# A Perceiver layer on one core: scores by pairs of heads, a fused decay and maximum, quantization shared with GpSimd, and the tail's weights loaded early

## The reference

```python
x = x + cross_attention(layernorm(x), ctx)        # 16 heads of 64, 4096 keys, biases, @ Wo + bo
x = x + self_attention(layernorm(x))              # 16 heads of 16, 256 keys
x = x + ffn(layernorm(x))                         # 256 -> 704 -> 256, silu(gate) * up
# self_attention
latent = (x @ W_k + x @ W_v) @ W_down_kv          # 64 wide
k, v   = latent @ W_up_k, latent @ W_up_v
scores = (q @ k.T) / sqrt(256) * exp(-0.01 * |i - j|)
out    = softmax(scores) @ v, all heads, @ W_o
# ffn: every product has both operands quantized to FP4 and back, in blocks of 16 along the last dim:
scale = max(|block|) / 6;  q = nearest of {0, .5, 1, 1.5, 2, 3, 4, 6} to |x / scale|, with sign, * scale
```

## Time and profile before

| | |
|---|---|
| runs | 1412.96, 1418.12, 1417.87 us, median 1417.87 |
| profiled execution | 1414.05 us, its span 1412.1 us |
| TensorE busy | 1315.2 us, 93% of the span |
| VectorE, ScalarE, GpSimd busy | 1006.2, 870.5, 657.0 us |
| TensorE's mean granted clock | 0.973 |
| read from HBM | 20.85 MB |

### The profile page before, as it was taken

One profiled execution on the slowest core, in us unless ns is written; L12 is line 12 of the kernel. 1 busy time (PEld: TensorE's weight loads), 2 busy tenths in 40 slices (PEclk: granted clock), 3 DMA queues, 4 the chain that ended last, 5 costly groups with the idle time before them and its releaser, 6 DMA issues. The chain is left out here.

```text
span 1412.1 us, 24618 instructions
## 1 busy us (share of the span) xinstructions
PE 1315.2 (93%) x9284; PEld 1121.4 (79%) x9284; DVE 1006.2 (71%) x1375; ACT 870.5 (62%) x1700; POOL 657.0 (47%) x797
## 2 busy tenths in 40 slices
PE   5899999999999999999999999999999996589857
PEld 5788888888888888888888888888888885267734
DVE  3666678667866777678767876787678767299666
ACT  3667666676667666676667666766676663256511
POOL 5655755475547553565457545754574440000000
PEclk9999999999999999999999999999999999699879
DMA  4010000000000000110000000000000000300000
GB/s 127 16 45 2 16 1 9 8 16 1 9 9 31 16 24 31 38 31 9 2 23 1 8 2 23 1 9 1 9 1 1 1 9 1 101 0 1 1 0 15
DMA packets 24901, 22.95 MB, mean 16 GB/s; under 512 B 4432, under 2 KB 24528, under 8 KB 24784
## 3 DMA queue, kind: packets, MB, share of 16 engines
q1 hardware_dynamic: 24784, 21.38, 5.0%
HBM read 20.85 MB, written 0.52 MB: 15 GB/s over the span
## 5 line engine op out<-in xcount | busy, mean ns | idle before, releaser
L548 ACT ACTIVATE pT_hi<-psT 128x512 fp32r<-128x512 f32 x512 | 292.4, 601 | 237.6 <-PE psT L320 222.5
L623 DVE TENSOR_TENSOR pT_lo<-psT,pT_hi 128x512 fp32r<-128x512 f32 x512 | 330.3, 684 | 105.4 <-ACT pT_hi L548 104.9
L617 DVE TENSOR_REDUCE negm<-psS 128x1 f32<-128x1024 f32 x256 | 311.7, 1218 | 51.2 <-PE psS L310 51.2
L267 POOL TENSOR_TENSOR kT<-kraw,khi 64x512 fp32r<-64x512 f32 x252 | 324.9, 1289 | 0.0
L513 ACT ACTIVATE prob<-psS,negm 128x1024 f32<-128x1024 f32 x256 | 285.7, 1116 | 1.0 <-DVE negm L617 1.0
L320 PE MATMUL psT<-ident,prob 128*128 128x128 f32 x2048 | 268.5, 274 | 3.9 <-DVE pT_lo L623 3.9
L261 POOL CAST khi<-kraw 128x512 fp32r<-128x512 f32 x126 | 76.9, 610 | 418.0 <-ACT kraw L523 416.6
L336 PE MATMUL psO<-pT_hi,v 128*128 128x256 f32 x1024 | 268.5, 294 | 1.2 <-DVE pT_lo L623 0.4
L320 PEld LDWEIGHTS psT<-ident,prob 128*128 128x128 f32 x2048 | 233.1, 140 | 38.8 <-issue 11.1
L337 PE MATMUL psO<-pT_lo,v 128*128 128x256 f32 x1024 | 256.7, 283 | 0.0
L336 PEld LDWEIGHTS psO<-pT_hi,v 128*128 128x128 f32 x1024 | 196.2, 192 | 2.7 <-DVE pT_lo L623 2.6
(11 more groups left out here) (215 smaller groups left out, 1563.9 us busy)
## 6 DMA issues: line engine op xcount, KB each, us to landing
cst<-in_ctx_dram SPq DMA_DIRECT2D x12, 512.0 KB, 3.8
oT<-in_ctx_dram SPq DMA_DIRECT2D x4, 512.0 KB, 5.3
wraw<-in_L_xattn_Wk_dram SPq DMA_DIRECT2D x8, 256.0 KB, 2.7
wraw<-in_L_xattn_Wv_dram SPq DMA_DIRECT2D x8, 256.0 KB, 2.7
wraw<-in_L_xattn_Wq_dram SPq DMA_DIRECT2D x8, 256.0 KB, 2.7
wo<-in_L_xattn_Wo_dram SPq DMA_DIRECT2D x8, 256.0 KB, 2.8
ff_wdn<-in_L_ffn_w_down_dram SPq DMA_DIRECT2D x1, 704.0 KB, 8.2
ff_win<-in_L_ffn_w_gate_dram SPq DMA_DIRECT2D x1, 640.0 KB, 5.3
```

The lines of the kernel that those rows point to most:

```text
L267: pool.tensor_tensor(kT[half, m // 2 % KRING, h, 1, :], raw[own, :], khi[own, :].bitcast(F32), ALU.subtract).then_inc(k_split, 1)
L548: act.activation(pT_hi[:, i % PRING, :], psT[:, t % 2, :], ACT.Copy).then_inc(ph_ok, 1)
L617: dve.tensor_reduce(negm[:, g % 2, h, qt, c:c + 1], psS[:, qt, :], AX.X, ALU.max, negate=True)\
L623: dve.tensor_tensor(pT_lo[:, i % PRING, :], psT[:, t % 2, :], pT_hi[:, i % PRING, :].bitcast(F32), ALU.subtract).then_inc(pl_ok, 1)
```

## The change

**Loads.** A class `Tail` holds the second part's weights in the memory that the transposed context takes in the first part; SyncE loads them once the last key and value projections are done (`k_ps`, `v_ps` at N), and no longer at the start of the second part. GpSimd makes masks and distances there, ScalarE the decay in steps 125 and 126. The output bias is loaded in the first group, and GpSimd adds it to y in step 12.
**Merged weights.** GpSimd adds W_k and W_v, TensorE turns the sum and multiplies it by W_down_kv after the loop; the latent is then one product of x (`wc`), and `kvT` is gone.
**Last group.** Its quarters 0 to 5 are merged within steps 125 to 127, one head a step, with the weights for a head made by itself (`head_max`, `head_end`); the sums of these six are three additions on GpSimd. Quarters 6 and 7 stay behind the loop, on VectorE.
**Scores.** q is masked by parity only; a head is a product over 32 rows, and the pair of heads of `scores(p)` has different rows. There are four PSUM banks, two for a pair. Weight turning takes PSUM space of `saO` that is free at the time, with one buffer instead of two.
**VectorE.** Decay and maximum are one `tensor_tensor_reduce` for each half of the queries, and the negation is an operation of its own. **Quantization.** Operations 0, 1, 2, 3, 5 and 6 of a chunk stay on VectorE at fixed heads, 4, 7, 8 and 9 go to GpSimd, with two buffers. The first batch is normalized in iteration 19, the second at the end.

```diff
+    # first part, GpSimd
+    if n == FIRST + KT * FIRST:
+        pool.tensor_tensor(y[:, :, :], y[:, :, :], cst[:, 0, :]...to_broadcast([P, B * QT, D]), ALU.add)
+    def add_out(g, k):
+        pool.tensor_tensor(oweighed[:, 0:2, :], oweighed[:, 0:2, :], oweighed[:, 2:4, :], ALU.add)
+        pool.tensor_tensor(oweighed[:, 0, :], oweighed[:, 0, :], oweighed[:, 1, :], ALU.add)
+        pool.tensor_tensor(on[:, qt, h * HD:(h + 1) * HD], oweighed[:, 0, 0:HD], oweighed[:, 0, HD:2 * HD], ALU.add)
+    # first part, TensorE: steps of the last group, then behind the loop
+    elif k >= 13 and g + 1 == GP:
+        wait(pe, comb, 16 * g + 2 * (2 * (k - 13) - 1) + 1 if k > 13 else 0)
+        post(g, 2 * (k - 13), psW[:, :])
...
+    if g == GP - 1 and k >= 13:
+        wait(pe, comb, 16 * g + 2 * 2 * (k - 13) + 1)
+        post(g, 2 * (k - 13) + 1, psW[:, :])
...
-    for k in range(8):
-        post(GP - 1, k, dst)
+    post(GP - 1, 6, psW[:, :])
+    post(GP - 1, 7, bank_S[0])
+    for half in range(KT):
+        for kt in range(KT):
+            last = pe.transpose(bank_T[0][...], tail.w[:, 0, kt, half * P:(half + 1) * P], ident[:, :])
+    for kt in range(KT):
+        for half in range(KT):
+            last = mm(bank_T[1][...], tail.wkvT[:, half, kt * P:(kt + 1) * P], tail.wd[:, half, :], ...)
+    # first part, VectorE, steps 13 to 15 of the last group
+    weigh_out(g, 2 * (k - 13), psW[:, :])       # before p_low(n, 0)
+    weigh_out(g, 2 * (k - 13) + 1, psW[:, :])   # before p_low(n, 2)
+    head_end(k - 12)                            # at the end of steps 12 to 15
+    head_max(k - 11)                            # at the end of steps 11 to 14
     # second part, TensorE
-    for d in range(KT):
-        step(("kv", d), product([(w[:, i, kt, cols(d)], xnT[:, kt, :]) for i in range(2) for kt in range(KT)]))
+    step(("lat", 0), product([(wc[:, kt, :], xnT[:, kt, :]) for kt in range(KT)]))
...
+    HEADS = (0, 2, 1, 3, 4, 6, 5, 7, 8, 10, 9, 11, 12, 14, 13, 15)
+    def scores(p):
+        if p >= 2:
+            pe.wait_ge(top_ok, 4 * p - 4)
+        for qt in range(QT):
+            for u in (2 * p, 2 * p + 1):
+                b, h = u // H, HEADS[u % H]
+                at = h % HPT // 2 * 2 * HD
+                rows = slice(at, at + 2 * HD)
+                last = mm(banks[u % 4][:, qt, :], qm[rows, h % 2, h // HPT, r * P:(r + 1) * P],
+                          kT[rows, h // HPT, b * S:(b + 1) * S], start=True, stop=True)
+        last.then_inc(s_ok, 1)
     for i in range(U + 3):
-        if i < U:
-            scores(i)
+        if i % 2 == 0 and i < U:
+            scores(i // 2)
     # second part, VectorE
+    CHUNK_AT = (0, 4, 9, 13, 18, 22)
     for u in range(U):
-        for i in range(WPU * u, min(WPU * u + WPU, CHUNKS * OPS)):
-            weight_op(i)
-        dve.tensor_tensor(sd_[:, u % 2, :, :], psS[:, u % 2, :, :], decay[:, :, :], ALU.mult)
-        dve.tensor_reduce(negm[:, u, :], sd_[:, u % 2, :, :], AX.X, ALU.max, negate=True)
+        for c in range(CHUNKS):                 # ops 0 | 1, 2, 3 | 5, 6 at CHUNK_AT[c] + 0 | 1 | 3
+            ...                                 # op 5 waits for GpSimd's op 4
+        if u == H + 3:
+            normalized(0)
+        for qt in range(QT):
+            dve.tensor_tensor_reduce(sd_[:, u % 2, qt, :], banks[u % 4][:, qt, :], decay[:, qt, :], 1.0,
+                                     -3.0e38, ALU.mult, ALU.max, top[:, u, qt:qt + 1])
+        dve.tensor_scalar(negm[:, u, :], top[:, u, :], -1.0, None, ALU.mult).then_inc(max_ok, 1)
+    # second part, GpSimd, for each chunk
+    pool.wait_ge(wq, 6 * c + 4)
+    pool.tensor_tensor(blocks(a), blocks(src), wide(wrs), ALU.mult).then_inc(wp, 1)       # op 4
+    pool.wait_ge(wq, 6 * c + 6)
+    pool.tensor_tensor(a, a, m, ALU.add).then_inc(wp, 1)                                  # op 7
+    pool.tensor_tensor(a, a, m, ALU.subtract).then_inc(wp, 1)                             # op 8
+    pool.tensor_tensor(blocks(src), blocks(a), wide(wamax), ALU.mult).then_inc(wp, 1)     # op 9
```

More of the change, by code:

```diff
@@ L185, in load_piece @@
                     wait(sp, prep_ps, u)
+                if b == 1 and piece == 0:
+                    wait(sp, bo_ok, 1)
                 sp.dma_start(cst[:, :, :], ctx_t[b, piece]).then_inc(cst_in, 16)
@@ new lines, in _ @@
+            SD, SH = D // 16, P * 16 // D
+            wait(pool, k_ps, N)
+            wait(pool, v_ps, N)
+            pool.memset(tail.win[:, :, tail.win.shape[2] - 1, :], 0.0).then_inc(tail.zero_ok, 1)
+            pool.memset(tail.hm[:, :], 1.0).then_inc(tail.const, 1)
+            pool.iota(tail.rel[:, :, :], [[P, QT], [-1, S]], base=0, channel_multiplier=1,
+                      allow_small_or_imprecise_dtypes=True).then_inc(tail.const, 1)
+            pool.wait_ge(tail.const, 2)
+            pool.affine_select(out=tail.hm[:, :], in_=tail.hm[:, :], compare_op=ALU.is_ge, fill=0.0, base=0,
+                               pattern=[[-SD, SH]], channel_multiplier=1).then_inc(tail.masks, 1)
@@ new lines, in _ @@
+            pool.wait_ge(tail.masks, 1)
+            pool.affine_select(out=tail.hm[:, :], in_=tail.hm[:, :], compare_op=ALU.is_ge, fill=0.0, base=SD - 1,
+                               pattern=[[SD, SH]], channel_multiplier=-1).then_inc(tail.masks, 1)
+            for k in range(6):
+                add_out(GP - 1, k)
+                if k == 1:
+                    wait(pool, tail.w_in[0], 16)
+                    wait(pool, tail.w_in[1], 16)
+                    pool.tensor_tensor(tail.w[:, 0, :, :], tail.w[:, 0, :, :], tail.w[:, 1, :, :], ALU.add)\
+                        .then_inc(tail.kv_ok, 1)
@@ L494, in _ @@
                     turn_ctx(u, cst, psW[:, :])
-            for k in range(8):
[L497 to L502, removed]
-                post(GP - 1, k, dst)
+            pe.wait_ge(comb, 16 * (GP - 1) + 2 * 5 + 1)
+            post(GP - 1, 6, psW[:, :])
+            pe.wait_ge(exp_ok, 2 * N)
+            post(GP - 1, 7, bank_S[0])
+            pe.wait_ge(tail.kv_ok, 1)
+            pe.wait_ge(pl_ok, 4 * N)
+            for half in range(KT):
+                for kt in range(KT):
+                    last = pe.transpose(bank_T[0][:, half * D + kt * P:half * D + (kt + 1) * P],
+                                        tail.w[:, 0, kt, half * P:(half + 1) * P], ident[:, :])
+            last.then_inc(tail.kvT_ps, 1)
+            pe.wait_ge(tail.kvT_ok, 1)
+            pe.wait_ge(tail.w_in[4], 16)
+            for kt in range(KT):
+                for half in range(KT):
+                    last = mm(bank_T[1][:, kt * HD:(kt + 1) * HD], tail.wkvT[:, half, kt * P:(kt + 1) * P],
+                              tail.wd[:, half, :], start=(half == 0), stop=(half == KT - 1))
+            last.then_inc(tail.wc_ps, 1)
             turn_o(GP - 1)
@@ L883, in _ @@
         def _(sp):
[L884 to L899, removed]
             for r in range(R):
@@ L1059, in _ @@
                     for kt in range(KT):
-                        last = mm(psS[:, half, j, :], oT[:, kt, r * P:(r + 1) * P], w[:, 3, kt, :],
+                        last = mm(banks[half][:, j, :], oT[:, kt, r * P:(r + 1) * P], w[:, 3, kt, :],
                                   start=(kt == 0), stop=(kt == KT - 1))
@@ L1304, in _ @@
                 rows = y[:, 2 * half:2 * half + 2, :]
-                dve.tensor_tensor(rows, psS[:, half, :, :], rows, ALU.add).then_inc(x1_ok, 1)
+                dve.tensor_tensor(rows, banks[half], rows, ALU.add).then_inc(x1_ok, 1)
             links = [0]
```

357 lines of the change are left out of this document (221 added, 136 removed).

## The result

The changed kernel takes 1420.7 us (median of 20 runs) against 1413.8 of the kernel before in the same rounds; the ratio is 1.0044, 95% interval 1.0035 to 1.0052. Forecast were 1389 us and a range from 1374 to 1403. The profiled execution has a span of 1419.4 us where before had 1412.1: 7.3 more. Two points in the traces already share out the difference. The first scores start at 1219.88 instead of 1242.61, so 22.7 us were gained ahead of the self-attention. They are lost within it, and more: its last values end at 1343.2 instead of 1336.5, 123.3 us after the first scores instead of 93.9. That is 29.4 more; the feed-forward part adds 0.6.

The account below looks back on a forecast made before the run. No engine is full behind the cross-attention loop, so each stretch was priced by its own chain. Terms -9.1, -5.4, -7.2, +0.6, -3.1, -0.7 give -24.9: from 1414.05 to 1389 us (chance 0.45), range 1374 to 1403.

Parts of the forecast that it names:

- end of cross-attention: Last head group's merge and output projection: six of eight merge pairs leave VectorE's tail, projection at 2.4 GHz; -9.1 us.
- Start of the second part: Before self-attention: bias transfer and additions leave the path, -5.4 us; projections shrink from 28 records to 12, -7.2 us.
- Self-attention: Stage from first scores to last values: fill, drain, 13 rings, port waits and weight copies sum to 90.8 against 93.9; -3.1 us.
- Everything else: Self-attention: the part of the repeating chain besides scores and the new VectorE work, taken as unchanged at 2.75 us a pair.
- the ring: Self-attention's repeating chain of scores, VectorE work, exponentials, block copy and values; 5.1 us per pair of heads after the change.
- 1.9 as a sign for "no overlap": Self-attention: the forecast would be wrong if the score records of a pair span 1.9 us.
- M: Self-attention: new VectorE work per pair, two fused multiply-and-maximum operations and a negation; 1.05 us taken, 0.98 to 1.6 possible.
- row groups: Rival for self-attention scores: row groups don't overlap, a pair's scores take 2.0 us, 10.5 us more, 1400 us; chance 0.15.
- half rate: Rival for self-attention: the fused operation runs at half rate, 8 us more, 1397 us; chance 0.10.
- The port: Self-attention: VectorE's negation waits out GpSimd operations on the shared port; 11 pairs x 0.55 = 6 us (0 to 20).
- GpSimd as the bound: Rival for self-attention: GpSimd's operations decide above 3.0 us each; at 4.5 the time is 1424 us, slower; chance 0.05.
- Normalization at the end: After self-attention: only the second batch is normalized there, two operations of 0.36 fewer; -0.7 us.

Follow-up runs that it names:

- e2: The kernel before with one change: score matmuls take the 32 rows that hold the head instead of all 128; 1474.9 us, ratio 1.041.
- e9: The changed kernel with a pair's two heads in different halves, 64 rows per score matmul, and the negation as a reduction; 1398.3 us, ratio 0.987.
- e7: e5 with the negation of the maximum done by a reduction over one element; 1379.2 us, ratio 0.974.
- e10: The changed kernel (32-row pairs) with the negation as a reduction and nothing else; 1419.7 us, ratio 1.0041.
- e5: The changed kernel with the scores part alone undone: one head per step, all 128 rows, 16 masks; 1386.2 us, ratio 0.979.
- e1: The changed kernel with paired score matmuls over all 128 rows instead of 32 (results wrong, only times of use); 1405.2 us, ratio 0.992.
- e12: e7 with the full-height scores of two heads together every second step; 1399.3 us, ratio 0.991.

## Why the prediction was wrong, by its own steps
- **What bounds the kernel; end of cross-attention (-9.1, and +0.6 in the loop).** Right in sum, partly by luck: the last addition to y starts at 1199.26 (1200.6 forecast), 9.7 us earlier than 1208.98 where 8.5 were forecast. Its parts were off both ways: the loop with the added bias grew by 1.6 us, not 4.2, and the output projection took 3.34 us, not 1.99, since the clock fell as it began.
- **Start of the second part (-5.4 and -7.2).** Right within 0.4 us: 13.0 us gained where 12.6 were forecast. The first scores start at 1219.9 (1221 forecast).
- **Self-attention (-3.1): the failed step.** It was +29.4. "Everything else is 5.13 - 0.97 - 1.41 = 2.75" was read at 2.4 GHz and carried into a stage whose work had changed. At 1.2 GHz the same records need 1.52 for 1.07 and 0.93 to 1.05 for 0.44, and the ring became a queue on TensorE. The price of the clock in this stage stood at no point of the sum, nor among the rivals (the sum priced the clock only for the projections, the range at -3 to +4 us); it stood in one clause at the end, "if the attention runs at 1.2 GHz because TensorE is busy only some three quarters of it", and even there with the wrong reason: it came with TensorE busy all the time. The Trainium skill (TensorE: Matmul & The Clock Gate, Part 1) ties the clock to how busy TensorE has been; by that alone TensorE at 54.00 of 54.00 us would run at 2.4 GHz, and the rows and e2 say otherwise.
- **Its terms, where the clock is there,** were good: eight records of a pair in 1.0 us (1.3 taken; 2.01 at 1.2 GHz, which is why 1.9 as a sign for "no overlap" would have misled), M = 0.98 (1.05), ring 5.12 (5.1) in e9. The rivals on row groups and on a half rate are out.
- **The port (6 us).** Right in kind: negations at 0.17 or up to 1.41 us. The size fits by luck. e7 gained 7 us by removing it, but mostly because the clock no longer fell in the fill; behind the fill the long negations cost some 2 us of the ring's time. In the changed kernel all of it was hidden by TensorE (e10).
- **GpSimd as the bound.** No: its additions took 1.81 us (1.9 forecast), the multiplications with a broadcast operand 1.50.
- **Normalization at the end (-0.7)** and the rest: +0.6 together.
- **The forecast itself.** The parts without the pairing come to 1386 (e5), and its attention takes 89.7 us where my sum had 90.8. That is agreement of a different kernel, and in part luck: full-height scores cost TensorE 1.9 us a pair, 0.6 more than in my ring and 0.9 more than the overlapped ones, and what sets the step there is TensorE, not the ring.

## What to carry to other kernels
TensorE's clock is an input of the sum, not a constant of the stage: before a duration at 2.4 GHz is carried over, ask whether the edit leaves as much full-height matmul work, spread as it was where the duration was read. Giving a head's scores all 128 rows, the unused ones masked with zeros, was faster here than 32 rows, by 60 us in the kernel before (e2) and by 34 in the changed one, where the heads also went from pairs back to one in each step (e5). And a small `tensor_scalar` on a ring beside a busy GpSimd is better written as a reduction.

## What the runs showed of the hardware that I had not expected
- TensorE without an idle moment for 135 us stays at 1.2 GHz with 32-row scores, turns and 16-column values (e2); with 128-row scores in the same order it goes back: the kernel before is at 0.57 from 1252 to 1256 and at 1.00 from 1256 to 1326. 64 rows in two overlapped halves lie between (e9), and so do full-height scores in lumps (e1, e12).
- Matmuls on two different 32-row groups overlap almost completely: in the changed kernel the first two pairs took 2.00 us for 16 records at 2.4 GHz, 0.125 each, where full-height records of 256 columns follow one another at 0.24 us (a head's four in 0.97).
- GpSimd's multiplication of 128x768 by one value for each 16 columns took 1495 ns, its addition of two full operands 1808. Whether the repeated value or the operation makes the difference isn't parted; the addition of the bias, repeated over the row tiles, took 2395 ns for 128x1024, as much a column as the full one.
- Fused decay and maximum (changed kernel) follow one another at 0.34 us for 128x256 (418 ns by itself) with the read of the accumulator (83 ns) hidden behind it.
- A reduction over one element, 155 ns (e7), is no slower than the 170 ns of the operation that it replaces (e5).
